# Drives of five of every eight scan units on ScalarE and TensorE, and half of their transposes ahead of the sum over n

## What is computed

```python
def step(h, inp):
    xt, dtt, Bt, Ct = inp
    dA = jnp.exp(dtt[:, :, None] * A)
    h = dA * h + (dtt * xt)[:, :, None] * Bt[:, None, :]
    y = jnp.einsum('ben,bn->be', h, Ct)
    return (h, y)
```

## Time and profile before

| what | value |
|---|---|
| median of three runs | 13,690.9 us |
| profiled execution, its own time | 13,708.09 us |
| its span | 13,706.3 us |
| instructions | 178,924 |
| scan units (16 bodies of 128) | 2,048 |
| of these driven by ScalarE, GpSimd and TensorE | 1,024 |
| one body, the eighth, from the scan of its unit 0 to that of the next | 833.6 us |

### The profile page before, as it was taken

The page is one execution under the profiler, slowest core; times in us unless marked ns, Lnnn a source line. Parts: engine busy times, 40 slices in busy tenths (PEclk is TensorE's granted clock), DMA queues, the critical chain, the costliest instruction groups (busy, mean ns, idle before and its releaser), DMA issues.

```text
span 13706.3 us, 178924 instructions
## 1 busy us (share of the span) xinstructions
PE 10481.0 (76%) x51212; PEld 5968.3 (44%) x51212; DVE 12472.7 (91%) x7742; ACT 10941.1 (80%) x23356; POOL 11259.0 (82%) x5316
## 2 busy tenths in 40 slices
PE   5667877778787787877777777787877878777776
PEld 2334444444343444444444444443444444444445
DVE  5999999999999999999999999999999999999991
ACT  6788888788787888878888788887878878788882
POOL 4888888888888888888888888888888888888891
PEclk7778888889898898988888898898988889889898
DMA  2223333333233333333323333332333333233232
GB/s 86 83 91 101 108 100 118 106 107 116 93 120 102 114 109 105 114 98 117 117 97 104 104 118 110 102 117 93 119 105 109 117 99 117 98 115 116 98 106 85
DMA packets 601084, 1450.50 MB, mean 106 GB/s; under 512 B 64016, under 2 KB 105120, under 8 KB 595504
## 3 DMA queue, kind: packets, MB, share of 16 engines
q1 hardware_dynamic: 599984, 1437.65, 31.8%
HBM read 1347.12 MB, written 90.28 MB: 105 GB/s over the span
## 4 chain that ended last, share of the span: by engine, by line
PE 26%; issue 23%; ACT 19%; DVE 16%; POOL 14%; DMA 1%; DVEq 0%; POOLq 0%; ACTq 0%; SPq 0%
POOL state L1244 11%; DVE state L1214 9%; PE driven L843 7%; ACT state L1023 6%; ACT v_sb L1036 6%; PE q_ps L798 6%; PE y_ps L857 4%; DVE driven L1203 2%; PE b_ps L833 2%; POOL v_sb L1276 2%; PE q_ps L785 2%; PE p_ps L706 1%; PE p_ps L714 1%; ACT L1023 1%; ACT hid L1006 1%
## 5 line engine op out<-in xcount | busy, mean ns | idle before, releaser
L1244 POOL TENSOR_TENSOR state<-state,c_rep 128x1024 f32<-128x1024 f32 x4096 | 9709.5, 2394 | 2011.9 <-DVE state L1214 2010.4
L1214 DVE TENSOR_TENSOR_SCAN state<-state,driven 128x1024 f32<-128x1024 f32 x4096 | 9104.6, 2271 | 581.8 <-PE driven L843 445.5
L1036 ACT ACTIVATE v_sb<-u_t,b_t 128x128 f32<-128x128 f32 x12288 | 3997.4, 506 | 1711.5 <-PE driven L843 1709.6
L1023 ACT ACTIVATE state<-ud_rep,cols_sb 128x512 f32<-128x512 f32 x8192 | 5191.1, 712 | 6.3 <-PE y_ps L857 3.2
L857 PE MATMUL y_ps<-state,consts_sb 128*32 128x512 f32 x16384 | 2534.4, 691 | 1824.2 <-POOL state L1244 1817.1
L843 PE MATMUL driven<-consts_sb,v_sb 128*128 128x128 f32 x16384 | 2712.2, 325 | 852.6 <-DVE state L1214 842.6
L843 PEld LDWEIGHTS driven<-consts_sb,v_sb 128*128 128x128 f32 x16384 | 2251.1, 168 | 2147.1 <-DVE state L1214 1704.8
L1203 DVE TENSOR_TENSOR driven<-ud_rep,b_ps 128x1024 f32<-128x1024 f32 x2048 | 2391.0, 1214 | 17.1 <-DMA ud_rep<-ud_rows 17.1
L798 PE MATMUL q_ps<-hid,wq_sb 128*128 128x256 f32 x8192 | 2130.4, 406 | 133.9 <-ACT hid L1001 80.0
L798 PEld LDWEIGHTS q_ps<-hid,wq_sb 128*128 128x128 f32 x8192 | 1535.7, 197 | 880.6 <-issue 647.2
L857 PEld LDWEIGHTS y_ps<-state,consts_sb 128*32 128x32 f32 x16384 | 341.5, 114 | 3003.5 <-POOL state L1244 2460.9
(11 more groups left out here) (115 smaller groups left out, 5646.0 us busy)
## 6 DMA issues: line engine op xcount, KB each, us to landing
c_rep<-bc_rows SPq DMA_DIRECT2D x2048, 256.0 KB, 3.0
ud_rep<-ud_rows SPq DMA_DIRECT2D x512, 512.0 KB, 4.1
wq_sb<-in_h SPq DMA_DIRECT2D x512, 512.0 KB, 3.9
wq_sb<-in_f SPq DMA_DIRECT2D x128, 512.0 KB, 4.6
wp_sb<-in_win SPq DMA_DIRECT2D x64, 512.0 KB, 4.6
dt_sb<-conv_taps SPq DMA_DIRECT2D x32, 1024.0 KB, 5.2
ud_rows<-u_pad SPq DMA_DIRECT2D x128, 256.0 KB, 3.4
ud_rows<-dt_sb SPq DMA_DIRECT2D x128, 256.0 KB, 3.4
```

What stands on the lines that cost most here:

```text
L1023: ins = act.activation(state[:, unit % STATE_RING, j, :], ud_rep[:, nth % 2, j, 1, :], ACT.Exp, scale=a_neg[:, d, c, j, g:g + 1])
L1036: ins = act.activation(v_sb[:, unit // 2 % V_RING, tt, :, :, n].rearrange("p j e -> p (j e)"), u_t[:, nth % 2, tt, :], ACT.Identity, scale ...
L1214: dve.tensor_tensor_scan(flat, flat, driven[:, q % DRIVE_RING].rearrange("p j t -> p (j t)"), 0.0, ALU.mult, ALU.add).then_inc(scanned, 1)
L1244: pool.tensor_tensor(part, part, c_rep[:, unit % ROW_RING, :].unsqueeze(1).to_broadcast([P, 2, T]), ALU.mult).then_inc(was_read, 1)
```

## The change

The units are taken in cycles of eight. In each cycle units 1, 2, 4, 5 and 7 are driven by way of v, the other three by VectorE; it was every second unit. `by_pe` says which way a unit goes, and `pe_units` and `dve_units` count the units of each kind ahead of one, for the slots of v and the semaphore counts. On TensorE the first half of a unit's transposes comes before the sum over n of unit u-1 and the second half behind it; where u is the first unit of a pass both stay behind the sum. Spreads of B are issued for the units that VectorE drives. On ScalarE the order of a unit u becomes: first half of the decays of u+2; last quarter (tt = 2) of v for u+2, middle quarter for u+3, first quarter for u+4, each if that unit is driven so; second half of the decays of u+2; side work. `V_AHEAD` goes from 5 to 4. GpSimd makes its quarter of v after the readings of u if u+3 is driven by way of v.

```diff
-DRIVE_RING, STATE_RING, ROW_RING, V_RING, V_AHEAD, POOL_AHEAD = 2, 4, 2, 2, 5, 3
-PE_UNITS = tuple(range(1, UNITS, 2))
-DVE_UNITS = tuple(range(0, UNITS, 2))
+DRIVE_RING, STATE_RING, ROW_RING, V_RING, V_AHEAD, POOL_AHEAD = 2, 4, 2, 2, 4, 3
+CYCLE, PE_OF_CYCLE = 8, (1, 2, 4, 5, 7)
...
+def by_pe(unit):
+    return unit % CYCLE in PE_OF_CYCLE
+
+def pe_units(unit):
+    return unit // CYCLE * len(PE_OF_CYCLE) + sum(k < unit % CYCLE for k in PE_OF_CYCLE)
+
+def dve_units(unit):
+    return unit - pe_units(unit)
...
         def v_free(at, unit):
-            return of_body(at, 2 * len(PE_UNITS), 2 * (unit // 2 - V_RING + 1)) + 2 * V_RING
+            return of_body(at, 2 * pe_units(UNITS), 2 * (pe_units(unit) - V_RING + 1)) + 2 * V_RING
...
                 for unit in range(UNITS):
                     before_scans = unit == 0 and at.kind in ("mid", "last", "tail")
+                    to_drive, ends_pass = scans and unit + 1 < UNITS and by_pe(unit + 1), unit % NG == 0
+                    if to_drive and not ends_pass:
+                        drive(at, unit + 1, 0)
                     if before_scans or scans and unit:
                         accumulate(at, unit - 1)
-                    if scans and unit + 1 in PE_UNITS:
+                    if to_drive and ends_pass:
                         drive(at, unit + 1, 0)
+                    if to_drive:
                         drive(at, unit + 1, 1)
-                        if unit + 2 < UNITS:
-                            spread(at, unit + 2)
-                        elif at.has("next"):
-                            spread(at, unit + 2)
+                    if not by_pe(unit + 2) and (scans if unit + 2 < UNITS else scans and at.has("next")):
+                        spread(at, unit + 2)
                     side(at, unit)
...
                 for unit in range(UNITS):
-                    if unit % 2 == 0:
-                        if in_scan(at, unit + 2):
-                            decays(at, unit + 2, 0)
-                            decays(at, unit + 2, 1)
-                        if in_scan(at, unit + V_AHEAD):
-                            make_v(at, unit + V_AHEAD, 0)
-                    else:
-                        if in_scan(at, unit + V_AHEAD - 1):
-                            make_v(at, unit + V_AHEAD - 1, 1)
-                        if in_scan(at, unit + 2):
-                            decays(at, unit + 2, 0)
-                            decays(at, unit + 2, 1)
+                    if in_scan(at, unit + 2):
+                        decays(at, unit + 2, 0)
+                    for tt in (2, 1, 0):
+                        ahead = unit + V_AHEAD - tt
+                        if by_pe(ahead) and in_scan(at, ahead):
+                            make_v(at, ahead, tt)
+                    if in_scan(at, unit + 2):
+                        decays(at, unit + 2, 1)
                     side(at, unit)
...
-                        if unit + 1 < UNITS and unit + 1 in DVE_UNITS or unit + 1 == UNITS and at.has("next"):
+                        if not by_pe(unit + 1) and (unit + 1 < UNITS or at.has("next")):
                             drive(at, unit + 1, 0)
                             drive(at, unit + 1, 1)
...
-                    if unit % 2 == 0 and (at.kind in SCAN_PARTS if ahead < UNITS else at.has("next")):
+                    if by_pe(ahead) and (at.kind in SCAN_PARTS if ahead < UNITS else at.has("next")):
                         make_v(at, ahead)
```

More of the change, by code:

```diff
@@ L395, in pe_drives @@
         def pe_drives(at, unit, h):
-            return of_body(at, 2 * len(PE_UNITS), 2 * (unit // 2) + h + 1) + 2 * V_RING
+            return of_body(at, 2 * pe_units(UNITS), 2 * pe_units(unit) + h + 1) + 2 * V_RING
         def v_free(at, unit):
-            return of_body(at, 2 * len(PE_UNITS), 2 * (unit // 2 - V_RING + 1)) + 2 * V_RING
+            return of_body(at, 2 * pe_units(UNITS), 2 * (pe_units(unit) - V_RING + 1)) + 2 * V_RING
         def v_count(at, unit):
-            return of_body(at, len(PE_UNITS), len([u for u in PE_UNITS if u <= unit]))
+            return of_body(at, pe_units(UNITS), pe_units(unit) + 1)
         def dve_drives(at, unit, h):
-            return of_body(at, 2 * len(DVE_UNITS), 2 * (unit // 2) + h + 1) + 1
+            return of_body(at, 2 * dve_units(UNITS), 2 * dve_units(unit) + h + 1) + 1
         def u_rows(unit):
@@ L843, in drive @@
                         mm = pe.transpose(driven[:, q % DRIVE_RING, j % 2, tt * P:(tt + 1) * P],
-                                          v_sb[:, unit // 2 % V_RING, tt, j].rearrange("p e n -> p (e n)"), ident)
+                                          v_sb[:, pe_units(unit) % V_RING, tt, j].rearrange("p e n -> p (e n)"), ident)
                 mm.then_inc(pe_driven, 1)
@@ L937, in step @@
                         if at.kind != "pre" and not (d and at.kind == "first"):
-                            act.wait_ge(b_spread, of_body(at, len(DVE_UNITS), 0 if d else len([u for u in DVE_UNITS if u < UNITS // 2])))
+                            act.wait_ge(b_spread, of_body(at, dve_units(UNITS), 0 if d else dve_units(UNITS // 2)))
                         act.activation(b_parts[d][:], p_ps[:], ACT.Copy).then_inc(done, 1)
@@ L946, in step @@
                         if at.kind != "pre" and not (d and at.kind == "first"):
-                            act.wait_ge(v_pooled, of_body(at, len(PE_UNITS), 0 if d else len(PE_UNITS) // 2))
+                            act.wait_ge(v_pooled, of_body(at, pe_units(UNITS), 0 if d else pe_units(UNITS // 2)))
                         act.activation(b_t[:, d].rearrange("p a n -> p (a n)"), p_ps[:, 0:TT * N], ACT.Copy).then_inc(done, 1)
@@ L981, in step @@
                     if nth > 1 or at.kind != "first":
-                        act.wait_ge(v_pooled, of_body(at, len(PE_UNITS), NG // 2 * (nth - 1)))
+                        act.wait_ge(v_pooled, of_body(at, pe_units(UNITS), pe_units(NG * (nth - 1))))
                     act.activation(u_t[:, int(name[2]) % 2].rearrange("p a e -> p (a e)"), p_ps[:], ACT.Copy).then_inc(done, 1)
@@ L1025, in decays, with make_v @@
                 ins.then_inc(decayed, 1)
-            def make_v(at, unit, part):
+            def make_v(at, unit, tt):
                 nth, g = unit % UNITS // NG, unit % NG
-                if part == 0:
+                if tt == 0:
                     act.wait_ge(pe_driven, v_free(at, unit))
-                    if g == 1:
+                    if g == PE_OF_CYCLE[0]:
                         act.wait_ge(act_side.sem, act_side.done(at, "o0" if nth else "next", f"UT{nth}")
                                     if nth or unit >= UNITS else act_side.before(at))
-                for tt in (2, 1) if part else (0,):
-                    for n in range(NN):
-                        ins = act.activation(v_sb[:, unit // 2 % V_RING, tt, :, :, n].rearrange("p j e -> p (j e)"),
-                                             u_t[:, nth % 2, tt, :], ACT.Identity,
-                                             scale=b_t[:, nth // EC, tt, NN * g + n:NN * g + n + 1])
-                if part:
+                for n in range(NN):
+                    ins = act.activation(v_sb[:, pe_units(unit) % V_RING, tt, :, :, n].rearrange("p j e -> p (j e)"),
+                                         u_t[:, nth % 2, tt, :], ACT.Identity,
+                                         scale=b_t[:, nth // EC, tt, NN * g + n:NN * g + n + 1])
+                if tt == TT - 2:
                     ins.then_inc(v_made, 1)
@@ L1200, in drive @@
                         dve.wait_ge(ud_in[nth % 2], pass_loaded(at, unit // NG))
-                    dve.wait_ge(b_spread, of_body(at, len(DVE_UNITS), unit // 2 + 1))
+                    dve.wait_ge(b_spread, of_body(at, dve_units(UNITS), dve_units(unit) + 1))
                 dve.wait_ge(scanned, of_body(at, HALVES, 2 * unit + h - DRIVE_RING + 1) + DRIVE_RING)
@@ L1208, in scan @@
                 dve.wait_ge(decayed, of_body(at, HALVES, q + 1))
-                if unit in DVE_UNITS:
+                if not by_pe(unit):
                     dve.wait_ge(dve_driven, dve_drives(at, unit, h))
@@ L1273, in make_v @@
                 pool.wait_ge(pe_driven, v_free(at, unit))
-                if g == 1:
+                if g == PE_OF_CYCLE[0]:
                     pool.wait_ge(act_side.sem, act_side.done(at, "o0" if nth else "next", f"UT{nth}"))
-                pool.tensor_tensor(v_sb[:, unit // 2 % V_RING, TT - 1].rearrange("p j e n -> p (j e) n"),
+                pool.tensor_tensor(v_sb[:, pe_units(unit) % V_RING, TT - 1].rearrange("p j e n -> p (j e) n"),
                                    u_t[:, nth % 2, TT - 1, :].unsqueeze(2).to_broadcast([P, P, NN]),
```

2 lines of the change are left out of this document (added).

## The result

The changed kernel takes 13,738.4 us (median of 7 runs, 13,729.5 to 13,751.6); the kernel before took 13,690.2 us on the same chip. The ratio is 1.0036, 95% interval 1.0027 to 1.0046: 48 us or 0.36% slower, where 79 us over the median shown before, or 0.6%, was forecast.

A forecast was written before the change was run, and what follows sets the result against it. VectorE, 91% busy, was first suspect, leading 12 of 16 stretches; the change hands the bottleneck to three engines. 5.1 us per body over 16 bodies, 82 us, on 13,690.9 gives 13,773, forecast as 13,770 us; range 13,310 to 14,090.

The forecast's parts named there:

- The four engines' totals: Busy time per loop body after the change: VectorE 741.7 us, ScalarE 743.2, GpSimd 720.8, TensorE 680.
- The price of an added unit: ScalarE's 12 scaled copies for one more driven unit, taken as 3.75 us per eight units, with 3.90 the other bound.
- The floors of the stretches: Largest engine busy time in each of 16 eight-unit stretches of the body, summing to 799.9 us against 790.3.
- Between stretches of 8 and of 16: Loop body's added time: 9.6 us by eight-unit stretches, 0.6 by sixteen; the middle, 5.1 us per body, 82 us, taken.
- I cost the move at zero: TensorE's first half of transposes ahead of the sum: gain at most 445.5 us, half-clock price 1.4 us per unit, netted to zero.
- rival 4: TensorE's second half of transposes, behind the sum, reaches scans late at half clock: 14,275 us, or 14,025 if half; chance 0.18.
- The coupling, held constant at 43.3 us per body: Loop body time beyond the summed largest busy times, 833.6 us against 790.3, assumed unchanged; called the forecast's weakest term.
- rival 1: Scans' 445.5 us wait for transposes goes through the early half: 13,328 us, or 13,550 if half; chance 0.25.
- rival 2: VectorE stays the bound everywhere, ScalarE's new work fitting its 1,709.6 us of waiting for v: 13,092 us; chance 0.13.
- rival 3: It evens out: 16-unit stretches are right, or a little gain on the wait meets added work: 13,690 us; chance 0.12.
- v late: Sign the forecast is right: scans wait more than today for transposes that waited for v; no size given.
- The rule weighed: TensorE transposes at the skill's 275 ns each would add 104 us in all; the trace's 0.136 us was used instead.

The follow-up runs named there:

- e4: The changed kernel with nine of ScalarE's twelve scaled copies of v per driven unit, the rest filled once at the start: 13,515.5 us.
- e3: The changed kernel with four of eight units (1, 3, 5, 7) driven by way of v, keeping the new orders: 13,599.0 us.
- e1: The changed kernel with both halves of a unit's transposes behind the sum again, still five of eight units: 13,872.7 us.
- e5: The kernel of e3 with both halves of the transposes behind the sum; differs from the kernel before by ScalarE's order and V_AHEAD alone: 13,657.5 us.
- m4: The changed kernel with the share set stretch by stretch, three to five of eight (68 driven units per body): 13,487.5 us.
- m1: The changed kernel with the share set stretch by stretch, four to six of eight (72 driven units per body): 13,813.2 us.
- e6: The changed kernel with GpSimd's product of v over one of four tiles, the others filled once with zeros: 13,664.4 us.

## Why the prediction was right

The sign held, and so did the part of the mechanism that e4 tests: ScalarE's load sets much of the pace. That the size came out near is in part luck. A gain of 90 us that was put at zero and a share that cost 139 us for 82 met in the sum.

**The four engines' totals.** VectorE was to come to 741.7 us per body and ScalarE to 743.2; they are 747.2 and 733.8. GpSimd was to have 720.8 and has 717.8. TensorE stays at 650.9 where 680 was worked out; its granted clock rose from 0.86 to 0.89 over the body. ScalarE's busy time rose by 50.6 us per body, not 60. The price of an added unit was right all the same: from e3 to the changed kernel, which differ by the share alone, it rose by 943.5 us for 256 units, 3.69 us each for the 3.75 taken. What the sum left out is that the new order makes ScalarE less busy, by 126.7 us from the kernel before to e3.

**The floors of the stretches.** The seventh was to go over 47 us and went to 49.0, the sixteenth from 50.9 to over 52.3 and went to 54.8, the fourteenth to stay at 61.5 or above and went to 63.6; the second and third were to become shorter by 1 to 3 us; the third did, by 1.8, the second by 0.7 only. The eleventh was to pass 47 and didn't: ScalarE has 44.56 us there for 47.03. The ninth was to become shorter and became longer, 59.6 for 58.9, with VectorE busy for 57.93 us of it: one small instruction there took 6.55 us. Over the loop the ninth is 59.0 us for 58.4, and the four small instructions of its norm take 6.5 us where it was 1.7, more than the 2.34 of drives that it lost; of this more at the end. The sixth was to have room, with GpSimd leading at 52.08 of 58.4. It grew to 60.0 with GpSimd at 43.84 and ScalarE at 49.42; VectorE waits there for ScalarE's side work, 6.6 us per body over the loop for the 2.2 of before. TensorE was to lead in the thirteenth and fifteenth; in the changed kernel it leads in none.

**Between stretches of 8 and of 16.** Here the size was off. I took the middle, 5.1 us per body, 82 us. e3 against the changed kernel measures the share alone: 139 us, 8.7 us per body, or 11.3 in the bodies of the loop. That is near the 9.6 of eight-unit stretches, but it doesn't show that these sums were right. Added up from each kernel's own busy times over the loop, the largest of each stretch come to 791.2 us before, 796.9 in e3 and 795.0 in the changed kernel. The sum didn't rise with the share, and it moved by 5.7 us with the orders alone, at the same work. By stretch the sixth and ninth grew by 3.5 and 0.9 us from e3 to the changed kernel, where they were to shrink by 1.6 and 2.3; the fifth, seventh, eleventh, fourteenth and sixteenth grew by 7.8 us together where 16.1 was forecast. And for e4 the same sums gave 370 us and 223 were measured.

**"I cost the move at zero."** This step failed. The early half of the transposes gains 134 us at five of eight (e1), against a bound of 445.5, and 58 at four (e3, e5); ScalarE's new order, to which I gave no gain either, adds 30. Gain and price weren't of one size: beside e1 the scans' waits before the first half fall by 414 us, and 234 come up before the second. The price is there as it was worked out, 1.47 us for the 1.4 at half clock, but it is paid less often than rival 4 had it. The parts are -90 us for the orders and +139 for the share. That they add to the measured +48 is no check, since e3 stands in both differences. The forecast's +82 had both too near to zero.

**The coupling, held constant at 43.3 us per body.** Against the forecast's sums it is 37 for the changed kernel (837.2 us over the loop against 799.9) and 36 for e3 (825.9 against 790.3). Used with 36.5 it gave m4 within 8 us, and it failed for m1, where it is 62. Against each kernel's own sums it reads otherwise: 42.9 before, 42.2 in the changed kernel, 29.0 in e3, 35.8 in e5, 50.9 in e1, 37.5 in m4 and 58.6 in m1. So the changed kernel kept its coupling; the sum was too high, 3.8 us more over the loop for 9.6. What the orders gain (42.9 to 29.0) and what the share costs (29.0 to 42.2) both show in the coupling and not in the sum of the floors. It is no constant of this kernel; here the two changes of it happened to cancel.

**The rivals.** The scans' wait for transposes didn't go, it doubled (rival 1), though the early half does shorten it (e1 has 1,062.8). ScalarE's work didn't vanish into its waiting for v (rival 2): that fell by 505 us while its busy time rose by 817. An even outcome (rival 3) missed by 21 us. The late half (rival 4) is a cost, but 234.1 us of waiting and not the 502 of its full price, and the early half gains more. Of the scans' other waits for transposes the largest part, 395 us, comes with v late, within TensorE's 444.3 us of waiting for it. I had listed that as a sign and given it no price.

**The rule weighed.** One transpose lasts 316 ns in the changed kernel's records (325 before), near the 275 of the Trainium skill (TensorE: Matmul & The Clock Gate, Part 4: PE-mode transpose). But transposes overlap: 20,480 of them kept TensorE busy for 3,321.6 us, 0.162 us each, and that is what they add to its busy time. By the Trainium skill's figure TensorE would lead in five stretches, and it leads in none.

## What to carry to other kernels

When the busiest engine (91% of the span here) has three others close behind it (76 to 82%) and the rings between them are two to four slots, cut a body into stretches of a few units and add up the largest busy time of each. That sum is a first estimate of what moving work is worth, better than the averages over the span, and no more than that: it gave 370 us for a relief that brought 223, it moved by 5.7 us a body with an order alone, and where it came near, some stretches missed up as others missed down. Then move work only in the stretches in which the receiver has room: five of eight everywhere lost 48 us, five of eight in five of the sixteen stretches, with three in one and the new orders, gained 200, of which the orders alone gave 90 (e3). Don't price one part of a change by another: try the orders at the old share and the share at the old orders, since here a gain of 90 us was hidden behind a cost of 139.

## What I had not expected

The ninth stretch of the changed kernel has this in its timeline (GpSimd and VectorE alone):

```profile
6397.15 4.65 POOL L1256 TENSOR_TENSOR state<-state,c_rep 128x1024 f32<-128x1024 f32 x2
...
6400.92 6.55 DVE L1159 SCALAR_TENSOR_TENSOR small<-small 128x4 f32<-128x4 f32 x1 [0.44 <-ACT small L928]
6401.77 1.03 POOL L1288 TENSOR_TENSOR v_sb<-u_t,b_t 128x512 f32<-128x512 f32 x1
...
6402.77 4.68 POOL L1256 TENSOR_TENSOR state<-state,c_rep 128x1024 f32<-128x1024 f32 x2
6407.51 0.17 DVE L1160 TENSOR_TENSOR small<-small 128x4 f32<-128x4 f32 x1
```

A VectorE instruction on 128x4 elements with both inputs in SBUF began at 6400.92, while a reading of GpSimd was under way, and ended at 6407.47, right behind the last of three more GpSimd instructions that followed one another without a gap, at 6407.45. Over the run the same instruction takes (minimum/median/maximum ns), in the kernel before and then in the changed one:

```profile
L1147 DVE SCALAR_TENSOR_TENSOR small<-small x64: 166/502/1818, 40.7 to 13442.3; 128x4 f32<-128x4 f32 x64
```

```profile
L1159 DVE SCALAR_TENSOR_TENSOR small<-small x64: 166/698/6553, 40.9 to 13474.0; 128x4 f32<-128x4 f32 x64
```

It is no single case. Of its 64 executions 46 took over 300 ns in the changed kernel, and each of these ended 20 to 28 ns behind the end of a GpSimd instruction; in the kernel before it was 51 of 51. The Trainium skill (SBUF — State Buffer, Who interferes with whom) says that a VectorE instruction with two SBUF inputs contends with a GpSimd instruction that reads SBUF, and calls the port pair that they share an exclusive lock. The trace agrees, and shows that the wait can outlast one instruction of GpSimd. The instruction two behind it (L1161), which has one tensor input, is held as well: 14 of its 64 executions took 2.29 to 2.30 us for a median of 0.17 and ended 26 to 33 ns behind GpSimd, where before the change one took 0.97. In e6, where GpSimd's product is short, the mean of the first instruction is 610 ns for 893 in the changed kernel. What all this costs over the run wasn't tested by itself.

The mean granted clock of TensorE went up, from 0.862 to 0.883 over the span, and its busy time rose by 59 us only for 4,096 more transposes. About half of that rise came with the orders: e3, with no transpose more than the kernel before, has 0.872. In the second stretch it went from 0.61 to 0.79 and the busy time fell from 40.09 to 34.35 us, with 11 more matmuls.

One driven unit more in a row makes a large difference: two in a row left the second stretch at 55.8 us for 56.6, three made it 61.2.
